# Signals of PE's products in a four-layer graph kernel: one for each product, or one for a group

## The reference

```
x = layernorm(x + L0(x))   # attention with 8 heads: exp(clip(K[src].Q[dst]/4)) weights V[src], summed by dst; then a feed-forward net
x = layernorm(x + L1(x))   # attention with 4 heads and a softmax over each node's edges, gated skip
x = layernorm(x + L2(x))   # four GCN convolutions
x = layernorm(x + L3(x))   # two GIN convolutions
```

## Time and profile before

| what | value |
|---|---|
| median of 3 plain runs | 5887.75 us (5886.36 to 5898.59) |
| the profiled execution, its span | 6640.4 us |
| attention sweep, in the profile | 1495 us |
| score sweep | 1475 us |
| leftover counting | 94 us |
| dense stage | 2240 us |

### The profile page before, as it was taken

The page is one execution under the profiler, slowest core; times in us unless marked ns, Lnnn a source line. Parts: engine busy times, 40 slices in busy tenths (PEclk is TensorE's granted clock), DMA queues, the critical chain, the costliest instruction groups (busy, mean ns, idle before and its releaser), DMA issues. The chain is left out here.

```text
span 6640.4 us, 100472 instructions
## 1 busy us (share of the span) xinstructions
PE 4599.9 (69%) x23624; PEld 3812.1 (57%) x23625; DVE 3837.8 (58%) x9293; ACT 2210.7 (33%) x4021; POOL 2644.9 (40%) x2513
## 2 busy tenths in 40 slices
PE   4455565565555455555555466549999999999997
PEld 2344444444322233333332355449999999999997
DVE  5466666666545566656566888864444466444443
ACT  0132223232212333333334133224444444334432
POOL 0355555555104565555550000014444444334432
PEclk7777777777787667666676676669999999999999
DMA  0333333333114455555552133233434344323332
GB/s 19 113 88 88 90 89 88 89 88 88 46 50 127 138 151 149 149 145 149 145 145 67 52 103 103 83 107 147 148 142 147 143 171 158 117 107 146 133 129 79
DMA packets 543144, 750.30 MB, mean 113 GB/s; under 512 B 57967, under 2 KB 441966, under 8 KB 542734
## 3 DMA queue, kind: packets, MB, share of 16 engines
q1 hardware_dynamic: 461182, 521.35, 23.4%
q0 software_dynamic: 81552, 224.63, 12.3%
HBM read 584.36 MB, written 161.41 MB: 112 GB/s over the span
## 5 line engine op out<-in xcount | busy, mean ns | idle before, releaser
L557 POOL DMA_INDIRECT arena<-table_kv,arena x1664 | 1684.5, 1012 | 1427.2 <-DVE arena L801 434.5
L2190 PE MATMUL ps<-moving,parts 128*128 128x384 f32 (+1 forms) x11662 | 2016.5, 331 | 38.2 <-ACT moving L2252 20.4
L2190 PEld LDWEIGHTS ps<-moving,parts 128*128 128x128 f32 x11662 | 1950.0, 188 | 71.9 <-ACT moving L2252 29.4
L2131 POOL CAST moving<-counts 128x1152 fp32r<-128x1152 uint8 (+1 forms) x420 | 476.7, 1135 | 1544.7 <-DVE counts L2265 935.6
L311 PE MATMUL ps<-by_place,by_lo 128*128 128x392 bf16 x1568 | 659.5, 525 | 438.7 <-issue 197.3
L320 ACT ACTIVATE counted<-ps 128x392 uint8<-128x392 f32 x1568 | 682.1, 506 | 619.7 <-PE ps L311 276.7
L2131 POOL CAST moving<-big 128x1152 fp32r<-128x1152 uint8 (+1 forms) x413 | 468.4, 1134 | 610.2 <-PE ps L2190 610.2
L667 PE MATMUL ps<-arena 128*128 128x137 f32 x1664 | 350.6, 372 | 370.1 <-DVE arena L801 358.5
L311 PEld LDWEIGHTS ps<-by_place,by_lo 128*128 128x128 bf16 x1568 | 190.0, 126 | 679.3 <-issue 433.9
L301 DVE TENSOR_TENSOR slots<-slots,counted 128x196 uint16 x1568 | 406.3, 259 | 289.0 <-issue 218.1
L667 PEld LDWEIGHTS ps<-arena 128*128 128x128 f32 x1664 | 301.2, 261 | 403.4 <-DVE big L764 190.0
(11 more groups left out here) (291 smaller groups left out, 5326.6 us busy)
## 6 DMA issues: line engine op xcount, KB each, us to landing
counts<-adjacency SPq DMA_DIRECT2D x53, 2352.0 KB, 8.5
big<-adjacency SPq DMA_DIRECT2D x52, 2352.0 KB, 8.6
adjacency<-slots SPq DMA_DIRECT2D x784, 98.0 KB
edge_values<-arena SPq DMA_DIRECT2D x208, 256.0 KB
arena<-edge_values SPq DMA_DIRECT2D x208, 256.0 KB, 3.1
arena<-table_kv,arena POOLq DMA_INDIRECT x1664
big<-table_norm SPq DMA_DIRECT2D x60, 192.0 KB, 5.7
big<-adjacency SPq DMA_DIRECT2D x7, 1568.0 KB, 6.5
```

The source lines that it names most:

```text
L557: pool.indirect_dma_start(m.ring4[r][:, k * 2 * D:(k + 1) * 2 * D], None, table, bass.IndirectOffsetOnAxis(m.src[:, j * HALF + k:j * HALF ...
L2131: pool.tensor_copy(to, of).then_inc(by_pool, 1)
L2190: mm = pe.matmul(m.bank(g % 2, n * P), d.parts[SOURCE[u]][:, s + q, t_, :], moving[:, q * n * P:(q + 1) * n * P], start=(s + q == 0 and t_ ...
```

## The change

Four attention products of a half raise `used` once, at the last product, in place of one each, and all waits on `used` are divided by four. Of the counting products, those with an odd number in their group raise `product`, so it counts pairs; `count_move` waits for the pair that holds its step, and `count_lo` for half the number that it had. Instructions, tables, order and data are the same.

```diff
--- before.py
+++ after.py
@@ -265,7 +265,7 @@
 def count_lo(dve, ct, c, r):
 
 
-    wait(dve, ct.product, (c - 1) * HALF)
+    wait(dve, ct.product, (c - 1) * (HALF // 2))
     dve.tensor_tensor(ct.by_lo[:, r % 2], ct.fours[:, 0:P, :], copies(ct.lo[:, ds(c * HALF, HALF)], 1, P), ALU.is_equal)
 
 
@@ -308,7 +308,9 @@
     if k == 0:
         pe.wait_ge(ct.hot, c + 1)
     wait(pe, ct.moved, c * HALF + k - banks + 1)
-    pe.matmul(m.bank(bank, WIDE), ct.by_lo[:, r % 2, :, k], ct.by_place[:, r % 2, :, k], start=True, stop=True).then_inc(ct.product, 1)
+    mm = pe.matmul(m.bank(bank, WIDE), ct.by_lo[:, r % 2, :, k], ct.by_place[:, r % 2, :, k], start=True, stop=True)
+    if k % 2:
+        mm.then_inc(ct.product, 1)
 
 
 def count_move(act, m, ct, c, r, k, bank):
@@ -316,7 +318,7 @@
 
     s = c * HALF + k
     wait(act, ct.added, s - 2 * HALF + 1)
-    act.wait_ge(ct.product, s + 1)
+    act.wait_ge(ct.product, c * (HALF // 2) + k // 2 + 1)
     act.activation(ct.counted[:, r % 2, k, :], m.bank(bank, WIDE), ACT.Copy).then_inc(ct.moved, 1)
 
 
@@ -665,7 +667,7 @@
                 pe.wait_ge(added, (j + 1) * HALF)
                 for k in range(HALF):
                     mm = pe.matmul(summed(k), m.hit[:, r % 2, k, :], m.msg[:, r % 2, k, :], start=True, stop=True)
-                    mm.then_inc(used, 1)
+                mm.then_inc(used, 1)
 
             def turn(j, r):
                 pe.wait_ge(hit_ready, j + 1)
@@ -688,7 +690,7 @@
                 products(j, r)
                 queries(j + 2, r % 2, at)
 
-            pe.sem_inc(used, HALF)
+            pe.sem_inc(used, 1)
             turn(0, 0)
             turn(1, 1)
             queries(0, 0, load_blocks(pe, regs, m, 0))
@@ -708,12 +710,12 @@
 
             def convert(j, r):
                 act.wait_ge(hit_ready, j + 1)
-                wait(act, used, j * HALF)
+                wait(act, used, j)
                 act.activation(m.hit[:, r % 2], m.hit16[:, r].rearrange("p n k -> p k n"), ACT.Copy).then_inc(converted, 1)
 
             def exps(j, h):
                 act.wait_ge(clipped, j + 1)
-                wait(act, used, j * HALF)
+                wait(act, used, j)
                 act.activation(m.msg[:, h, :, D:D + H0], raw[:, h].rearrange("p (k n) -> p k n", k=HALF),
                                ACT.Exp, scale=float(C0) ** -0.5).then_inc(weights_ready, 1)
 
@@ -759,7 +761,7 @@
                     if first:
                         return
                     to = m.sums[:, ds(at[k] * A0, A0)]
-                    dve.wait_ge(used, (j + 1) * HALF)
+                    dve.wait_ge(used, j + 1)
                     dve.wait_ge(added, j * HALF + k)
                     dve.tensor_tensor(to, to, summed(k), ALU.add).then_inc(added, 1)
 
@@ -819,7 +821,7 @@
             at = load_blocks(dve, regs, m, (2 * TURNS - 1) * HALF)
             for k in range(HALF):
                 to = m.sums[:, ds(at[k] * A0, A0)]
-                dve.wait_ge(used, (2 * TURNS + 1) * HALF)
+                dve.wait_ge(used, 2 * TURNS + 1)
                 dve.wait_ge(added, 2 * TURNS * HALF + k)
                 dve.tensor_tensor(to, to, summed(k), ALU.add).then_inc(added, 1)
```

## The result

The changed kernel takes 5907.67 us (median of 11 runs, 5895.90 to 5916.84), the kernel before 5889.95 us in the same series: 17.7 us slower, ratio 1.0027 with the interval 1.0019 to 1.0035. The forecast was 5894 us and no difference that can be told. The time lies in the range of 5862 to 5925, but outside the 5885 to 5903 that the prediction gave its likeliest case, and the loss is near three times the 6.5 us of its sum: a small loss that is clear of noise.

What follows compares the result with a forecast made beforehand. It took plain sweeps to run close to the gathers' pace, GpSimd first, VectorE's loop just behind in the attention sweep. Terms 0 + 0 + 0 + 6.5 us on 5887.75 gave 5894 us; range 5862 to 5925, likeliest case 5885 to 5903.

Steps and rivals of the forecast that it cites:

- The leftover counting: Counting left after the sweeps, 28 groups: moves up to 0.345 us later delay adds, 6.5 us slower (0 to 9.7).
- The matmuls: Matmuls themselves: signalling products are no slower than others, so 0, ends 3 us either way.
- the attention products' signal: Attention sweep: waiters already waited for a half's fourth signal, which comes at the same place, so 0.
- The counting in the score sweep: Score sweep: moves come up to 0.345 us later but are hidden, 0; without cover 72 us.
- the 3.46 us before the add: Score sweep: adds come 3.46 us after their moves begin, as VectorE adds a group one iteration behind; claimed cover.
- The counting in the attention sweep: Attention sweep: moves start 1.7 us after the second product is over, so later signals cost 0; without cover 72 us.
- The reading of the surplus: Profile 752.65 us over the plain median: laid mostly to profiling in the sweeps, plain runs at 5.33 us a half turn.
- rival A: Block adds' 376.7 us of remote waits are late, piled-up PE signals; fewer signals come sooner: 5826 us, chance 0.11.
- Rival B: Attention sweep: shorter signal tail, the last of four signals comes sooner and VectorE's loop gains: 5876 us, chance 0.09.
- rival C: Score sweep: the pair wait shows, 208 moves each cost 0.345 us, 72 us: 5966 us, chance 0.10.
- rival D: Small slower: leftover stage loses 9.7 us and either sweep a few more, near 5903 us, chance 0.10.

Runs made afterwards that it cites:

- the variant with the old numbers: Changed kernel, but each signal raises its semaphore by what it stands for, so waits keep the earlier kernel's numbers: 1.0005 of the kernel before, 5896.34 us.

## Why the prediction was right and wrong

*The leftover counting* was the term of the sum, 6.5 us in bounds of 0 and 9.7. By the first and last move it measures 82.7 us before and 90.1 after (2791.5 to 2881.6), 7.4 us, and 7.3 by the stage table. The mechanism was right (moves 0.90 us after the product, where 0.56 + 0.345 = 0.905 was to be expected). The share given to each sort of group, read from three groups, was a little low.

*The matmuls* (0) and *the attention products' signal* (0) were right: L669 busy as before, and the variant with both sweeps' signals thinned and nothing else changed is level. By this the Trainium skill's rule on the semaphore tail (TensorE: Matmul & The Clock Gate, section The cost: per-tile semaphore tail), from which an estimate of 16 us of gain was made, gives nothing here: 1352 fewer signals are 0.9 us by the medians, in an interval of 1.8 us slower to 8.8 faster. The page prices the signals of matmuls that end together. Here the instructions of the attention products start some 0.12 us apart on a fast chip, and only every second one signalled, so the signals came some 0.24 us apart.

*The counting in the score sweep* (0) was right, at 1.0001. That the moves are later there and cost nothing is shown; that the 3.46 us before the add are what hides them was not tested by itself.

*The counting in the attention sweep* (0) was wrong in its total and right in its reason: the later moves cost nothing there (1098.2 us with them, 1102.8 without), but the part had one more edit in it, the changed number of `count_lo`'s wait, and the prediction called VectorE's wait "as before". That is the step that failed: it put the changed number at nothing without a reason. The engines' own instructions are equal in number (9293 on VectorE in both), but the sequencer's are not, by 99 in VectorE's attention sweep. The number costs 7.3 us by the medians of the variant with the old numbers, 6.4 to 9 by the pairs in the attention sweep alone, and 6.8 by the lengths of the sweep. With the leftover's 7.4 that makes 14 to 16 of the 17.7 us, whose interval is 11 to 21; the changed kernel run again was 12.7 us slower by the medians. That the number is the cause is shown. By what path it lengthens the sweep is shown in part: VectorE has little room (it is busy 936.60 of 1098 us), but the gathers keep nearly the same pace. In the score sweep over 200 such instructions more cost nothing.

*The reading of the surplus* was wrong. The 752.65 us were put down to the profiler and to plain runs at 5.33 us a half turn. The number came out right (the attention sweep's mean is 1102.8 / 208 = 5.30, the score's 5.45), since the surplus does lie in the sweeps, but not the cause: by all that the later profiles show, the profile and the plain runs came from different chips. On the slow chip the long waits before the block adds are there in plain runs too, as span and plain time agree. Idle time before the block adds, attention sweep, kernel before on the slow chip, then on the fast:

```profile
L764 DVE TENSOR_TENSOR big<-big,ps 128x137 f32 x828 | 246.3, 297 | 421.9 <-remote 389.2 <-PE ps L667 21.6 <-issue 0.4
```

```profile
L764 DVE TENSOR_TENSOR big<-big,ps 128x137 f32 x828 | 245.0, 296 | 22.5 <-PE ps L667 11.3
```

So the wait that rival A had in view is real. That it is a wait for late signals of PE no run shows, since the profile can't name what ends it, and A's remedy did not help: with a quarter of the attention signals that chip was 1.0019 slower, not faster. Rival B shows nowhere, rival C is excluded by the pairs in the score sweep alone, and rival D, small and slower, is what came; it named no cause for its "few more" in a sweep.

What stays open: why the attention part alone costs 12 us on the slow chip (6 at least by the interval) and at most 8 on a fast one; its single profile there has the attention sweep 5 us shorter and the score sweep, in which nothing is changed, 27 us longer, which is the scatter of that chip and no answer. Open too is whether ScalarE's stream, which was also changed by the new numbers, has a part in the 7 us. It can hardly be a direct one, as VectorE waits for ScalarE no more than this in the attention sweep of the changed kernel, and just as little in the kernel before (there L801 for L717):

```profile
DVE arena L803 <- ACT arena L719: 0.3, 1, 0.3
```

And what makes the slow chip slow is open: it was seen in one series on one chip.

## What to carry to other kernels

A signal at a matmul costs nothing worth saving here. What thinning costs is decided by who stands directly behind the product, and by whether the number of a wait is still one that the engine has at hand; the second counts only in a stretch that this engine helps to pace. When signals are thinned all the same, raise the semaphore by what the signal stands for, so that every wait keeps its number, and keep single signals where the consumer stands directly behind. Edits of a wait's number belong in a prediction as a term of their own. Before a surplus of a profile over the plain time is put down to the profiler, ask for the kernel's own plain time on the chip of the profile.

## What the runs showed that was not expected

Chips differ: the same kernel takes 5889.95, 5895.32 and 5890.97 us in three series and 6673.61 us in a fourth, with all the difference in the two sweeps that gather (attention sweep 1517.7 against 1102.8 us, score sweep 1495.0 against 1133.0), while the stages from the end of the leftover counting on take 3025.0 and 3022.7 us. And a changed number in one wait, which adds an instruction of 45 ns to each of some 100 groups, can be seen in the time of a 5890 us kernel, though twice as many of them in the next sweep can't.
